# The head of a routed-expert block: the second bias as one row and two matmuls in place of a broadcast transfer

## The chip, the cores and the metric

The kernel runs on one core of one Trainium2 chip. The metric is device time in microseconds (us) of the whole program, the median of several runs.

## The reference, cut to what matters

The block takes 2048 tokens of width 128 and does three things in a row: an expert layer, a linear attention with its own small layer, and the same expert layer again. The expert layer, with `x` the normalised tokens, 8 experts, hidden width 512 and one expert per token:

```
logits = x @ router_W + router_b
probs  = softmax(logits);  gates = one_hot(argmax(probs)) * probs
h = relu(x @ W1[e] + b1[e])          # 512 wide
y = h @ W2[e] + b2[e]                # 128 wide
out = sum over e of gates * y
```

`b2` holds 8 rows of 128 numbers, one per expert: 4 KB. All data is float32.

## The kernel before, in words

The tokens are 16 tiles of 128, in 4 groups of 4 tiles. **Head.** SP issues, one after the other on its own queue, the four groups of `x` (256 KB each, line 411), `rb` (412), the first bias as 32 rows `eb1r` (413), the second bias `b2` (414), the first expert weights of 2 MB (415) and five of eight second weights of 256 KB each (416, helper at 372). The tile `ew` holds, for each partition and expert, W1, b1, b2 and W2 side by side; `B2_AT:W2_AT` is the piece for b2. Line 414 reads the 4 KB of b2 once for each of the 128 partitions, so 512 KB arrive. VectorE (DVE) takes statistics of each group (`begin0`), GpSimd (POOL) makes the reciprocal deviations (542) and a row of constants, TensorE (PE) turns each group by four transposes (`turn_xn`, 951) into a PSUM bank, and ScalarE (ACT) copies that bank to SBUF (`take_xn`, 729). PE then makes the router logits of the group (`logits`, 982). In the first two rounds of that loop (lines 1148 to 1156) stands a `keep_warm(1)`: one bf16 matmul of 512 columns whose result in bank 2 nobody reads. After group 1 PE turns `eb1r` (1156), which DVE copies to `ew` (1604).

**Routing.** DVE picks an expert per token in two halves (`pick(0, 0, 2)`, `pick(0, 2, 2)`, lines 1342 to 1366; each ends in the one-hot tile `oh`). PE's `ranks` (985 to 1017) waits for the first half and for ten constants of POOL, then counts; inside it a `keep_warm(1)` stands between the first half's counts and the `hits` matmul (1004). `tile_list`, a register load of the list of experts, and `sources` (1085) follow; DVE's `list_sources` (1391) writes `srcu`, the row numbers of each tile of the sorted list of 23 tiles.

**Gathers.** Meanwhile ACT (and POOL for group 2, line 589) makes the normalised rows `xn` (`renormalise`, 786) and ACT stores each group to DRAM (`store_xn`, 794, on ACT's queue). POOL then waits for the four stores (622), for `srcu` (623), and gathers the rows of one tile after another by indirect transfers (617). SP loads each tile's W1, b1 and b2 from `ew` into a ring of 8 (`load_weights`, 424), after `ew_in` (both loads into `ew`) and `ebias_ready`.

**Experts.** For each of the 23 tiles PE transposes the gathered rows (1103), multiplies by W1 (1110) and W2 (1127); ACT does the ReLU (755), DVE adds b2 (1473) from the ring. Attention and the second expert layer follow; there b2 is read from `ew` again, halved by POOL (701). Which work goes where and in which order is written out by hand; each engine follows its own list.

Of the kernel before, what the change touches and what calls it, by code (L numbers as in the profile page):

```python
# [5 lines left out]
P = 128  # L6
D = 128
# [5 lines left out]
NG = T // GT  # L13
NE = 8
F = 512
FC = F // P
# [40 lines left out]

W1_AT, B1_AT, B2_AT, W2_AT, EW = 0, F, F + FC, F + FC + D, F + FC + D + FC * D
CW = W2_AT


def bc(ap, shape):
# [3 lines left out]
def macaron_kernel(nc, x_d, g1_d, b1_d, wq_d, wk_d, wv_d, wo_d, g2_d, b2_d, w1_d, w2_d,  # L66
# [3 lines left out]
    ALU, ACT, AX = mybir.AluOpType, mybir.ActivationFunctionType, mybir.AxisListType.X  # L70
# [14 lines left out]
    with ctx:  # L85
# [3 lines left out]
        def sem(name):  # L89
            return ctx.enter_context(nc.semaphore(name))  # L90
# [3 lines left out]
        xi = sb("xi", [P, T, D])  # L94
# [118 lines left out]
        w_in = sem("w_in")  # L213
        ffw_in = sem("ffw_in")
        ew_in = sem("ew_in")
        const_ready = sem("const_ready")
        pool_chain = sem("pool_chain")
        dve_chain = sem("dve_chain")
        ebias_ready = sem("ebias_ready")
        rwmean_ps = sem("rwmean_ps")  # L220
        rwc_ready = sem("rwc_ready")
        eb1_T = sem("eb1_T")
        stats_ready = sem("stats_ready")
        rstd_ready = sem("rstd_ready")
        shift_ready = sem("shift_ready")
# [182 lines left out]
        @block.sync  # L408
        def _(sp):
            for g in range(NG):  # L410
                sp.dma_start(x[:, g * GT:(g + 1) * GT, :], x_v[:, g, :, :]).then_inc(x_in[g], 16)
            sp.dma_start(rb[:, :], rb_d.unsqueeze(0).broadcast_to([P, NE])).then_inc(rb_in, 16)
            sp.dma_start(eb1r[:, :], eb1_d.rearrange("e (c p) -> (e c) p", p=P)).then_inc(eb_in, 16)
            sp.dma_start(ew[:, :, B2_AT:W2_AT], eb2_d.unsqueeze(0).broadcast_to([P, NE, D])).then_inc(ew_in, 16)
            sp.dma_start(ew[:, :, W1_AT:W1_AT + F], ew1_d.rearrange("e p f -> p e f")).then_inc(ew_in, 16)
            load_w2(sp, range(NE - W2_BY_ACT))
            attention_weights = [(gb[:, j:j + 1], v.rearrange("(d a) -> d a", a=1))
                                 for j, v in enumerate((g1_d, b1_d, g2_d, b2_d))]
            attention_weights += [(wkv[:, 0:D], wk_d), (wkv[:, D:2 * D], wv_d), (wq[:, :], wq_d), (wo[:, :], wo_d),
                                  (w1[:, :], w1_d), (w2[:, :, :], w2_d.rearrange("(c p) d -> p c d", p=P))]  # L420

            def load_weights(t, e):

                sp.dma_start(ewc[t.ahead], ew[:, bass.ds(e, 1), 0:CW].squeeze(1)).then_inc(ewc_in[t.ahead], 16)

            def store_slots(k):

                sp.dma_start(slot_scr_v[:, k, :], ysb[:, k, :]).then_inc(y_stored[group_of(k)], 16)

            sp.wait_ge(whole_ready, 1)  # L430
            codes = load_list(sp, codei[0:1, 0:NT], NE * TPE - 1)
            sp.wait_ge(ew_in, 16 * 2)
            sp.wait_ge(ebias_ready, 1)
            for k in range(NT):
                t = Tile(k)
                if k == 1:
                    sp.wait_ge(g_in[0], 16)
                if k >= FIRST:
                    sp.wait_ge(xg_T, max(1, k - LEAD))
                if k >= UNROLL:  # L440
                    sp.wait_ge(y_ready, 1 + k - UNROLL)
                    store_slots(k - UNROLL)
                load_weights(t, expert_of(codes[k]))
            for n, k in enumerate(range(NT - UNROLL, NT)):
                sp.wait_ge(y_ready, 1 + k)
                store_slots(k)
                for out, src in attention_weights[2 * n:2 * n + 2]:
                    sp.dma_start(out, src).then_inc(w_in if n < 4 else ffw_in, 16)

            sp.wait_ge(fill_ready, FILL_PARTS)  # L450
            sp.wait_ge(yb_in[NG - 1], 16 * GT)
            for at in range(0, FILL, T * D):
                n = min(T * D, FILL - at)
                sp.dma_start(row_fill_v[:, at:at + n], xn[:, :, :].rearrange("p t d -> p (t d)")[:, 0:n]).then_inc(fill_done, 16)

            sp.wait_ge(list_ready, 1)
            first = load_list(sp, lists[0:1, 1, 0:FIRST], NE - 1)
            sp.wait_ge(b2_halved, 1)
            for k in range(FIRST):
                load_weights(Tile(k), first[k])  # L460
            sp.wait_ge(codes_ready, 1)
            codes = load_list(sp, lists[0:1, 0, 0:NT], CODES - 1)
            for k in range(FIRST, NT):
                t = Tile(k)
                if k == FIRST + 1:
                    for g in range(NG):
                        sp.wait_ge(scattered[g], 16 * GT)
                    for n in range(SURE, UNROLL):
                        load_rows(sp, Tile(n), codes[n])
                if k >= UNROLL:  # L470
                    sp.wait_ge(out_done[t.ahead], 16 * t.round)
                    load_rows(sp, t, codes[k])
                    sp.wait_ge(o_ready, 1 + k - UNROLL)
                sp.wait_ge(xg_T, NT + max(1, k - LEAD))
                load_weights(t, expert_of(codes[k]))
            for u in range(UNROLL):
                sp.wait_ge(out_done[u], 16 * uses(u))
# [246 lines left out]
        def _(act):  # L724
            A = nc.scalar.activation

            def take_xn(m, g):
                act.wait_ge(xnT_ps, m * NG + g + 1)
                A(xnT[:, g * GT:(g + 1) * GT, :], bank[xn_bank(m, g)][:, :], ACT.Copy).then_inc(xnT_ready, 1)

            def take_last_xn():

                for n, bk in enumerate((0, 4)):
                    act.wait_ge(xnT_ps, 2 * NG + n)
                    A(xnT[:, T - GT + 2 * n:T - GT + 2 * n + 2, :], bank[bk][:, 2 * n * P:(2 * n + 2) * P], ACT.Copy
                      ).then_inc(xnT_ready, 1)

            def exponentials():
                act.wait_ge(lg_ready, picks(0))
                A(ex[:, :, :], lg[:, :, :], ACT.Exp).then_inc(ex_ready, 1)  # L740
# [41 lines left out]
            def renormalise(g):  # L782

                act.wait_ge(shift_ready, g + 1)
                for t in range(g * GT, (g + 1) * GT):
                    last = A(xn[:, t, :], x[:, t, :], ACT.Identity, scale=rstd[:, t, 0:1], bias=shift[:, t, 0:1])
                last.then_inc(xn_ready, 1)

            def store_xn(g):
                if g == POOL_ROWS:  # L790
                    act.wait_ge(xn_by_pool, 1)
                else:
                    act.wait_ge(xn_ready, 1 + g - (g > POOL_ROWS))
                act.dma_start(xn_scr_v[:, g, :, :], xn[:, g * GT:(g + 1) * GT, :]).then_inc(xn_stored[g], 16)
# [12 lines left out]

            act.dma_start(rw[:, :], rw_d).then_inc(rw_in, 16)
            nc.scalar.preload_act_table_set("natural_log_exp_and_others")
            for g in range(NG):  # L810
                take_xn(0, g)
            renormalise(0)
            renormalise(1)
            store_xn(0)
            store_xn(1)
            renormalise(3)
            store_xn(3)
            store_xn(POOL_ROWS)
# [109 lines left out]
        def _(pe):  # L928
# [11 lines left out]
            def turn_xn(m, g):  # L940
# [11 lines left out]
                                               pay[:, t, 0:D] if m else x[:, t, :], ident[:, :])  # L952
                last.then_inc(xnT_ps, 1)

            def turn_last(j):

                pe.wait_ge(x3_ready, x3_count(B - 1, j))
                if j == 0:
                    pe.wait_ge(xnT_ready, 2 * NG - 1)
                turned = nc.tensor.transpose(bank[0 if j < 2 else 4][:, j * P:(j + 1) * P],  # L960
                                             pay[:, T - GT + j, 0:D], ident[:, :])
                if j % 2 == 1:
                    turned.then_inc(xnT_ps, 1)
# [21 lines left out]
            def ranks():  # L985
# [13 lines left out]
                mm(R[:, 0:PICKED * NE], before[:, :], oh[:, 0:PICKED, :], start=False, stop=False, skip_group_check=True)  # L999
                for t in range(PICKED):  # L1000
                    spread(t)
                keep_warm(1)
                pe.wait_ge(oh_ready, picks(0))
                mm(bank[4][:, 4:5], oh[:, :, :].rearrange("p t e -> p (t e)"), ones_bf[:, 0:1], start=True, stop=True
# [138 lines left out]

            turn_xn(0, 0)
            pe.wait_ge(rw_in, 16)
            mm(bank[4][:, 0:NE], avg[:, :], rw[:, :], start=True, stop=True).then_inc(rwmean_ps, 1)
            turn_xn(0, 1)
            for g in range(NG):
                if g + 2 < NG:
                    turn_xn(0, g + 2)  # L1150
                if g < 2:
                    keep_warm(1)
                logits(0, g)
                if g == 1:
                    pe.wait_ge(eb_in, 16)
                    nc.tensor.transpose(bank[7][:, 0:NE * FC], eb1r[:, :], ident[0:NE * FC, 0:NE * FC]).then_inc(eb1_T, 1)
            ranks()
            tile_list()
            keep_warm(5)
# [157 lines left out]
        def _(dve):  # L1317
# [273 lines left out]
            v.tensor_scalar(sums[:, :, :], sums[:, :, :], 1.0 / P, None, ALU.mult).then_inc(sums_ready, 1)  # L1591
            begin0(0)
            begin0(1)
            dve.wait_ge(rwmean_ps, 1)
            v.tensor_tensor(out=rwc[:, :], in0=rw[:, :], in1=bank[4][:, 0:NE], op=ALU.subtract).then_inc(rwc_ready, 1)
            first_shift(0)
            begin0(2)
# [2 lines left out]
            dve.wait_ge(rb_in, 16)  # L1600
            pick(0, 0, 2)
            first_shift(2)
            dve.wait_ge(eb1_T, 1)
            v.tensor_copy(ew[:, :, B1_AT:B2_AT], bank[7][:, 0:NE * FC].rearrange("p (e c) -> p e c", c=FC)
                          ).then_inc(ebias_ready, 1)
            pick(0, 2, 2)
# [188 lines left out]
```

## Time and profile before

| what | value |
|---|---|
| median of 3 runs | 205.19 us (204.97 to 207.0) |
| the profiled execution | 204.63 us |
| its span, first to last instruction | 202.9 us |
| PE, POOL, DVE, ACT busy | 185.8, 121.6, 122.7, 111.7 us |
| mean granted TensorE clock | 0.966 |

A chain of waits is read backwards from the last instruction; in the timeline a row is a start, a duration, an engine, a line and, in brackets, the idle time before it and what ended it. A float32 matmul shows as two matmul instructions. [...]

### The profile page before, as it was taken

What the parts mean: (1) busy time and instruction counts of PE and PEld (TensorE: products, weight loads), DVE (VectorE), ACT (ScalarE), POOL (GpSimd) and SP (SyncE); (2) the same over time, 40 slices, a digit from 0 to 9 for tenths busy, and PEclk for the clock granted to TensorE, in tenths of its full rate; (3) what the DMA queues carried; (4) which work ended last, traced back from release to release, by engine and by line L of the source; (5) the groups of instructions that cost most, each with busy time, mean ns of one, the idle gap of its engine ahead of it and who ended that gap; (6) DMA issues with size and microseconds to landing.
All of it is one profiled execution on the core that took longest, in us unless ns stands there. A gap on an engine that the chain in (4) does not pass through costs nothing.

```text
span 202.9 us, 4566 instructions
## 1 busy us (share of the span) xinstructions
PE 185.8 (92%) x1410; PEld 156.9 (77%) x1410; DVE 122.7 (60%) x521; ACT 111.7 (55%) x326; POOL 121.6 (60%) x186
## 2 busy tenths in 40 slices
PE   4969879999999998998999999998998999999992
PEld 2854358999999986777855868797545999999991
DVE  4868412222222888898897484876515677777762
ACT  2675026556556658787878852510302766766670
POOL 6887656587774576361887440858771354554554
PEclk9975599999999999999999999999999999999999
DMA  6999869767698562599990000011047867674700
GB/s 204 233 387 345 263 220 365 262 216 237 207 193 301 140 178 53 198 417 413 415 393 14 2 3 0 30 42 47 28 134 254 287 247 265 225 261 159 272 29 0
DMA packets 26680, 40.26 MB, mean 198 GB/s; under 512 B 4229, under 2 KB 16296, under 8 KB 25632
## 3 DMA queue, kind: packets, MB, share of 16 engines
q1 hardware_dynamic: 21136, 33.01, 46.2%
q0 software_dynamic: 2496, 4.76, 8.9%
q10 hardware_dynamic: 3024, 2.20, 3.5%
q8 instruction: 12, 0.20, 0.4%
q14 instruction: 12, 0.10, 0.1%
HBM read 10.78 MB, written 14.46 MB: 124 GB/s over the span
## 4 chain that ended last, share of the span: by engine, by line
PE 60%; DVE 17%; DMA 8%; POOL 7%; issue 4%; ACT 1%; ACTq 1%; POOLq 0%; DVEq 0%
PE bank L1110 18%; PE bank L1127 17%; PE bank L1248 7%; PE bank L1266 5%; DMA Xg<-xn_scratch,srcu 4%; PE bank L1103 3%; DMA xn_scratch<-xn 2%; PE bank L1201 2%; DMA eqrq<-row_scratch 2%; PE bank L934 2%; DVE stat L1335 2%; POOL xn L589 2%; PE bank L1211 1%; DVE x L1577 1%; PE bank L1218 1%
## 5 line engine op out<-in xcount | busy, mean ns | idle before, releaser
L755 ACT ACTIVATE hT<-bank,ewc_own 128x128 f32<-128x128 f32 x184 | 52.3, 368 | 48.9 <-PE bank L1110 48.8
L1110 PE MATMUL bank<-xT,ewc_own 128*128 128x128 f32 x368 | 48.7, 275 | 0.4 <-DVE xT L1467 0.3
L1127 PE MATMUL bank<-ew,hT 128*128 x368 | 48.5, 275 | 0.0
L1110 PEld LDWEIGHTS bank<-xT,ewc_own 128*128 128x128 f32 x368 | 44.7, 192 | 1.2 <-issue 1.2
L1127 PEld LDWEIGHTS bank<-ew,hT 128*128 128x128 f32 x368 | 44.7, 192 | 0.2 <-issue 0.2
L689 POOL DMA_INDIRECT out_dram<-ysb,eqrq x23 | 22.6, 983 | 25.4 <-DVE ysb L1477 25.1
L617 POOL DMA_INDIRECT Xg<-xn_scratch,srcu x23 | 22.0, 958 | 11.0 <-issue 5.8
L934 PE MATMUL bank<-ones_bf 128*128 128x512 bf16 x66 | 21.7, 464 | 3.1 <-POOL ident L507 2.7
L681 POOL DMA_INDIRECT row_scratch<-pay,posu x16 | 15.8, 987 | 11.0 <-DVE posu L1440 7.4
L1473 DVE TENSOR_TENSOR ysb<-bank,ewc_own 128x128 f32<-128x128 f32 x23 | 6.6, 289 | 26.0 <-PE bank L1127 24.6
L642 POOL DMA_INDIRECT xnT<-slot_scratch,posu x16 | 15.3, 958 | 9.4 <-DMA slot_scratch<-ysb 2.9
L1467 DVE COPY xT<-bank 128x128 f32<-128x128 f32 x46 | 13.1, 284 | 7.6 <-PE bank L1103 7.5
L1266 PE MATMUL bank<-w,actT 128*128 128x128 f32 x128 | 16.3, 278 | 0.0
L1103 PE MATMUL bank<-ident,Xg 128*128 128x128 f32 x46 | 12.8, 278 | 2.7 <-DMA Xg<-xn_scratch,srcu 1.9
L934 PEld LDWEIGHTS bank<-ones_bf 128*128 128x128 bf16 x66 | 6.9, 114 | 10.6 <-issue 5.0
L1266 PEld LDWEIGHTS bank<-w,actT 128*128 128x128 f32 x128 | 15.1, 192 | 0.0
L1248 PE MATMUL bank<-h1T,w 128*128 128x512 f32 x32 | 14.4, 592 | 0.0
L1477 DVE SCALAR_TENSOR_TENSOR ysb<-bank,gate,ysb 128x128 f32<-128x128 f32 x23 | 8.1, 351 | 9.6 <-PE bank L1127 8.9
L871 ACT ACTIVATE actT<-ewc_own 128x512 f32<-128x512 int16 x16 | 9.3, 622 | 8.0 <-DVE ewc_own L1678 8.0
L1486 DVE TENSOR_SCALAR Xg<-eqrq 128x128 f32<-128x128 f32 x23 | 7.9, 341 | 5.1 <-DMA eqrq<-row_scratch 5.0
L1248 PEld LDWEIGHTS bank<-h1T,w 128*128 128x128 f32 x32 | 5.8, 190 | 5.7 <-issue 5.5
L1678 DVE TENSOR_SCALAR ewc_own<-bank 128x512 int16<-128x512 f32 x16 | 10.0, 683 | 0.1
(240 smaller groups left out, 302.8 us busy)
## 6 DMA issues: line engine op xcount, KB each, us to landing
ewc_own<-ew SPq DMA_DIRECT2D x46, 322.0 KB, 3.4
row_scratch<-xn SPq DMA_DIRECT2D x8, 1024.0 KB, 10.6
ew<-in_L_ffn_W_dram SPq DMA_DIRECT2D x1, 2048.0 KB, 12.2
slot_scratch<-ysb SPq DMA_DIRECT2D x23, 64.0 KB, 3.3
ew<-in_L_ffn_W_dram SPq DMA_DIRECT2D x5, 256.0 KB, 9.3
eqrq<-row_scratch SPq DMA_DIRECT2D x18, 70.0 KB, 2.4
x<-in_L_attn_x_dram SPq DMA_DIRECT2D x4, 256.0 KB, 3.2
xn_scratch<-xn ACTq DMA_DIRECT2D x4, 256.0 KB, 5.7
```

What stands on the lines that cost most here:

```text
L617: g.indirect_dma_start(out=Xg[:, k % UNROLL, :], out_offset=None, in_=xn_scr, in_offset=bass.IndirectOffsetOnAxis(ap=srcu[:, k:k + 1], axis=0)
L642: g.indirect_dma_start(out=Yg[:, t, :], out_offset=None, in_=slot_scr[0:UPTO[group] * P, :], in_offset=bass.IndirectOffsetOnAxis(ap=posu[: ...
L681: g.indirect_dma_start(out=row_scr, out_offset=bass.IndirectOffsetOnAxis(ap=posu1[:, t:t + 1], axis=0), in_=pay[:, t, :], in_offset=None). ...
L689: g.indirect_dma_start(out=out_rows, in_=ysb[:, k, :], in_offset=None, bounds_check=TOK - 1, oob_is_err=False, out_offset=bass.IndirectOff ...
L755: last = A(hT[:, t.slot, c * P:(c + 1) * P], up_bank(k, c)[:, c * P:(c + 1) * P], ACT.Relu, scale=0.5 if m else 1.0, bias=ewc[t.ahead][:, ...
L934: mm(bank[2][:, :], ones_bf[:, :], bc(ones_bf[:, :].unsqueeze(1), [P, 4, P]), start=True, stop=True)
L1103: nc.tensor.transpose(bank[t.parity][:, 0:P], Xg[:, t.ahead, :], ident[:, :]).then_inc(xg_T, 1)
L1110: last = mm(up_bank(k, c)[:, c * P:(c + 1) * P], ewc[t.ahead][:, c * P:(c + 1) * P], xT[:, t.slot, :], start=True, stop=True)
L1127: last = mm(bank[4 + t.parity][:, 0:D], hT[:, t.slot, c * P:(c + 1) * P], ew[:, bass.ds(e[k], 1), W2_AT + c * D:W2_AT + (c + 1) * D].squee ...
L1248: mm(hidden_bank(c)[:, :], w1[:, c * P:(c + 1) * P], h1T[:, b % 2, :], start=True, stop=True).then_inc(u_ps, 1)
L1266: last = mm(row_bank(b, j)[:, j * P:(j + 1) * P], actT[:, b % 2, c, j * P:(j + 1) * P], w2[:, c, :], start=c == 0, stop=c == FC - 1)
L1467: v.tensor_copy(xT[:, t.slot, :], bank[t.parity][:, 0:P]).then_inc(xT_ready, 1)
```

## The change

Line 414 now loads b2 as one row of 4 KB into `xi`, a tile that is free until the attention, and counts on `eb_in` beside `eb1r`; `ew_in` counts the W1 load alone. PE spreads the row over the partitions by two float32 matmuls with a row of ones as weights (512 columns each, four experts at a time, into bank 2), and ACT copies bank 2 into `ew`. The first pair stands in round 0 of the logits loop and on ACT ahead of the copy of the last group, the second after that loop and on ACT after the first two stores are issued. The two `keep_warm(1)` of the loop are gone. The semaphores `rwmean_ps` and `eb1_T` become one, `small_ps`, which counts the router mean, the first spread, the turned `eb1r` and the second spread in PE's order.

```diff
-            sp.dma_start(ew[:, :, B2_AT:W2_AT], eb2_d.unsqueeze(0).broadcast_to([P, NE, D])).then_inc(ew_in, 16)
+            sp.dma_start(xi[0:1, 0:NE, :], eb2_d.unsqueeze(0)).then_inc(eb_in, 16)
...
-            sp.wait_ge(ew_in, 16 * 2)
+            sp.wait_ge(ew_in, 16)
+            sp.wait_ge(eb2_ready, 2)
...
+            def take_b2(n):
+                act.wait_ge(small_ps, 2 * (n + 1))
+                A(ew[:, n * HALF_E:(n + 1) * HALF_E, B2_AT:W2_AT], bank[2][:, :].rearrange("p (e d) -> p e d", d=D), ACT.Copy
+                  ).then_inc(eb2_ready, 1)
...
-            for g in range(NG):
+            for g in range(NG - 1):
                 take_xn(0, g)
+            take_b2(0)
+            take_xn(0, NG - 1)
             renormalise(0)
             renormalise(1)
             store_xn(0)
             store_xn(1)
+            take_b2(1)
             renormalise(3)
...
+            def spread_b2(n):
+                pe.wait_ge(eb_in, 16 * 2)
+                if n == 1:
+                    pe.wait_ge(eb2_ready, 1)
+                mm(bank[2][:, :], ones_v[0:1, :], xi[0:1, n * HALF_E:(n + 1) * HALF_E, :].rearrange("p e d -> p (e d)"),
+                   start=True, stop=True).then_inc(small_ps, 1)
...
                 for t in range(PICKED):
                     spread(t)
+                pe.wait_ge(eb2_ready, 2)
                 keep_warm(1)
...
-                if g < 2:
-                    keep_warm(1)
+                if g == 0:
+                    spread_b2(0)
                 logits(0, g)
                 if g == 1:
-                    pe.wait_ge(eb_in, 16)
-                    nc.tensor.transpose(bank[7][:, 0:NE * FC], eb1r[:, :], ident[0:NE * FC, 0:NE * FC]).then_inc(eb1_T, 1)
+                    pe.wait_ge(eb_in, 16 * 2)
+                    nc.tensor.transpose(bank[7][:, 0:NE * FC], eb1r[:, :], ident[0:NE * FC, 0:NE * FC]).then_inc(small_ps, 1)
+            spread_b2(1)
             ranks()
...
-            dve.wait_ge(eb1_T, 1)
+            dve.wait_ge(small_ps, 3)
```

## Rows read from the trace of the kernel before

**Rows 1.** Chain of waits, 16 to 40 us: start, duration, what.
```profile
16.54 4.97 DMA xn_scratch<-xn
...
22.08 0.04 POOLq L623
...
25.77 3.35 DMA Xg<-xn_scratch,srcu
...
29.50 0.92 PE bank L1110 x8
...
30.44 0.02 POOLq L612
```

**Rows 2.** Transfers of line 794, the store issued last alone.
```profile
L794 ACTq DMA_DIRECT2D xn_scratch<-xn x1: 327/327/327, 16.5 to 16.5; - x1
...
DMA to landing us min/median/max: 5.5/5.5/5.5
```

**Rows 3.** Timeline of DVE in the head: start, duration, line, operation.
```profile
9.83 0.23 DVE L1349 TENSOR_TENSOR lg<-bank,rstd 128x64 f32<-128x64 f32 x1 [0.49 <-PE bank L982]
...
13.26 0.22 DVE L1365 TENSOR_TENSOR oh<-key,kmax 128x64 bf16<-128x64 f32 x1
...
21.67 0.18 DVE L1391 TENSOR_SCALAR srcu<-bank 128x23 uint32<-128x23 f32 x1 [0.99 <-PE bank L1085]
```

**Rows 4.** Issues of transfers up to 45 us: queue, count, KB, us to landing.
```profile
ew<-in_L_ffn_b_dram SPq DMA_DIRECT2D x1, 512.0 KB, 6.3
...
eb1r<-in_L_ffn_b_dram SPq DMA_DIRECT2D x1, 16.0 KB, 3.2
```

**Rows 5.** Timeline of SP's queue, 3 to 21 us.
```profile
3.14 0.43 SPq L413 DMA_DIRECT2D eb1r<-in_L_ffn_b_dram  x1
3.62 0.42 SPq L414 DMA_DIRECT2D ew<-in_L_ffn_b_dram  x1
...
20.74 11.02 SPq L424 DMA_DIRECT2D ewc_own<-ew  x8
```

**Rows 6.** Stretches: engines' busy us and counts, then granted clock, DMA share, GB/s.
```profile
5.00:9.00 4.00, 3.83 (x33) 3.55 (x31) 3.73 (x24) 2.13 (x4) 3.39 (x6) 1.00 0.97 194
9.00:12.00 3.00, 2.69 (x23) 2.53 (x22) 2.27 (x15) 3.00 (x9) 2.35 (x8) 1.00 1.04 393
12.00:13.00 1.00, 0.00 (x0) 0.00 (x0) 0.87 (x4) 0.32 (x1) 0.71 (x5) 0.62 1.07 414
13.00:25.00 12.00, 10.72 (x65) 5.50 (x66) 7.03 (x30) 4.88 (x13) 9.16 (x19) 0.50 1.02 320
```

**Rows 7.** The page's costliest groups: the float32 matmul of 512 columns, later in the kernel.
```profile
L1248 PE MATMUL bank<-h1T,w 128*128 128x512 f32 x32 | 14.4, 592 | 0.0
```

**Rows 8.** Timeline of PE in the head.
```profile
6.96 0.38 PE L934 MATMUL bank<-ones_bf 128*128 128x512 bf16 x1
7.17 0.95 PE L982 MATMUL bank<-rwc,xnT 128*128 128x8 f32 x8
...
8.67 0.95 PE L982 MATMUL bank<-rwc,xnT 128*128 128x8 f32 x8
...
9.73 1.95 PE L982 MATMUL bank<-rwc,xnT 128*128 128x8 f32 x16
13.23 0.23 PE L990 MATMUL bank<-ones_v,whole 1*32 1x1 f32 x2 [1.54 <-POOL token L583]
...
14.37 0.61 PE L934 MATMUL bank<-ones_bf 128*128 128x512 bf16 x1
14.78 0.21 PE L1004 MATMUL bank<-ones_bf,oh 128*128 128x1 bf16 x1
14.92 0.61 PE L1006 MATMUL bank<-tileid,ones_v 1*128 1x23 f32 x2
```

**Rows 9.** Timeline of ACT in the head.
```profile
8.66 0.60 ACT L729 ACTIVATE xnT<-bank 128x512 f32<-128x512 f32 x1 [0.90 <-PE bank L951]
...
13.60 1.65 ACT L786 ACTIVATE xn<-x,shift,rstd 128x128 f32<-128x128 f32 x4 [1.28 <-DVE shift L1385]
```

More of the change, by code:

```diff
@@ L59 @@
 CW = W2_AT
+HALF_E = NE // 2
 def bc(ap, shape):
@@ L215, in macaron_kernel @@
         ew_in = sem("ew_in")
+        small_ps = sem("small_ps")
+        eb2_ready = sem("eb2_ready")
         const_ready = sem("const_ready")
@@ L219, in macaron_kernel @@
         ebias_ready = sem("ebias_ready")
-        rwmean_ps = sem("rwmean_ps")
         rwc_ready = sem("rwc_ready")
-        eb1_T = sem("eb1_T")
         stats_ready = sem("stats_ready")
@@ L1145, in _ @@
             pe.wait_ge(rw_in, 16)
-            mm(bank[4][:, 0:NE], avg[:, :], rw[:, :], start=True, stop=True).then_inc(rwmean_ps, 1)
+            mm(bank[4][:, 0:NE], avg[:, :], rw[:, :], start=True, stop=True).then_inc(small_ps, 1)
             turn_xn(0, 1)
@@ L1593, in _ @@
             begin0(1)
-            dve.wait_ge(rwmean_ps, 1)
+            dve.wait_ge(small_ps, 1)
             v.tensor_tensor(out=rwc[:, :], in0=rw[:, :], in1=bank[4][:, 0:NE], op=ALU.subtract).then_inc(rwc_ready, 1)
```

## Prediction, made before the changed kernel was run

> **What bounds the kernel now.** I read the chain of waits first. From 36 us on it is TensorE (PE) work nearly back to back, which the change doesn't touch; the head is what counts. There the chain goes through the last store of normalised rows, POOL's gathers and PE's first expert tiles [rows 1]. What delays the first gather delays the gathers behind it, PE's first tiles, and so the end, one for one.
>
> What releases the first gather? The store that is issued last starts at 16.54 and lands 5.5 us later, at 22.04 [rows 2]. POOL's record of the wait behind it, the one for `srcu`, stands at 22.08 [rows 1]. DVE finishes `srcu` at 21.67 + 0.18 = 21.85 [rows 3]. How long after its release such a record stands is seen further down: PE ends at 29.50 + 0.92 = 30.42, POOL's record is at 30.44 [rows 1]. So 22.08 fits a release at 22.04 and is 0.23 too late for one at 21.85. The store is the last wait, by 0.2 us only, and the routing that ends in `srcu` stands right behind it. That is the main reading: two paths, almost level, and the change helps one and touches the other.
>
> Second, the routing path. PE's `ranks` starts at 13.23 after 1.54 of idle time, released by POOL's constants, not by DVE; the `hits` matmul at 14.78 follows in PE's own order, while the second half of the one-hot tile was ready at 13.26 + 0.22 = 13.48 [rows 3, 8]. So PE has slack before 13.23, DVE has 1.3 us before 14.78, and work added on PE ahead of `ranks` is free up to 13.23 and costs one for one beyond.
>
> Third, the clock. It is 1.00 to 12 us, 0.62 on average from 12 to 13, and 0.50 after, up to 25 [rows 6]. A mean of 0.62 between 1.00 and 0.50 is 0.24 us at the upper level: it fell at 12.24, after PE went idle at 9.73 + 1.95 = 11.68 [rows 8].
>
> **The change part by part.** *Removed: the broadcast.* From 5 to 9 us the transfer engines are 97% busy yet move 194 GB/s; from 9 to 12 it is 393 [rows 6]. 4 us at 194 are 776 KB; less the 524 KB of the broadcast, 252 KB remain, 0.65 us at 393. So the broadcast took about 4 x 0.97 - 0.65 = 3.2 us of all engines. Were it as quick as the later transfers, 524 / 393 = 1.3. The transfers behind it move up by 1.3 to 3.2 us, I take 3.2, the row of its own stretch. The engines are full from 13 to 25 as well (share 1.02), so the last store feels it: it should land between 18.8 and 20.7 instead of 22.04. But only 0.2 of that is worth anything: after it `srcu` is late next. Gain: 0.2 us, with 0 as its other end.
>
> *Added on SP: one row.* It stands where the broadcast stood, so nothing is moved past a queue. Issued at 3.62 [rows 5], it should take what `eb1r`, 0.48 ahead of it in the same queue and four times as large, took: 3.2, landing at 6.8; the upper end is the broadcast's own 6.3, landing at 9.9 [rows 4]. PE arrives at 6.96 [rows 8]. I take 6.8 and no wait. SP's new wait for both copies stands ahead of its first weight load at 20.74 [rows 5]; the copies are done six us earlier (below): 0.
>
> *Added on PE: the first spread, in place of two warmers.* A float32 matmul of 512 columns is two instructions; 32 take 14.4 us, 0.45 each, and one lasts 592 ns to its end [rows 7]. So a spread holds PE for 0.90 and its result is there after 1.04. It starts at 6.96, where a warmer held PE for 7.17 - 6.96 = 0.21 [rows 8]: +0.69 for what follows. In the next round the other warmer's 0.21 goes: +0.48 from there on. The logits of group 3 end at 12.16 instead of 11.68; DVE's first pick starts at 10.3 instead of 9.83. Its cover is the 1.3 us before `hits`: 0.
>
> *Added on PE: the second spread.* It starts at about 12.05, as the last small matmul leaves PE. If the clock falls at 12.24 as now, 0.19 of its 0.90 run at the upper level and the other 0.71 take 1.42: PE is held to 13.66, the result is there at about 13.8. `ranks` starts at 13.66 instead of 13.23: **+0.43**. The ends: clock still up, 12.95, nothing; clock down before it, 12.05 + 1.80 = 13.85, +0.6. I take 0.43, since the fall is where the row has it.
>
> *Added on ACT.* The first copy (0.60, as a `take_xn` [rows 9]) runs from 8.0 to 8.65; the turned group 3 comes at 8.66 + 0.69 = 9.35 anyway, so it delays nothing by itself. The second waits for the second spread at 13.8 and ends at about 14.45. Behind it wait the rows of group 3, at 14.45 instead of 13.60 [rows 9], so its store is issued at 16.1; the last store still goes at 16.54, when POOL's rows are ready. Cover: 0.1 us of queue, and behind that the 1.3 to 3.2 us by which stores land earlier: 0. PE's new wait for this copy stands ahead of the warmer at 14.37 [rows 8], now 14.8, with `hits` queued behind it: 0.35 us of cover. DVE's wait for the turned `eb1r` is over by 10.3, before its pick ends: 0.
>
> *Sum.* `srcu` 0.43 later is 22.28; POOL passes at 22.30 instead of 22.08: +0.43 - 0.2 = **+0.2 us**, between -0.2 (second spread free) and +0.6 (clock down earlier, and no relief). Against the profiled execution that is 204.63 + 0.2 = 204.8. The median of the runs shown stands 0.56 above that execution, at 205.19, so I say 205.4.
>
> **The rivals.**
> 1. *The clock falls early, slower.* The warmers held the clock, and without them it falls before the logits are done. If it falls at t, all PE work from t to 12.05 takes twice its time and the second spread 1.80, so `ranks` starts at 13.85 + (12.05 - t). Less 0.2 of relief, the loss passes 1% (2.05 us) when t is before 10.4; at t = 9.0 it is 0.6 + 3.05 - 0.2 = 3.4, 208.6 us. For: the warmers are PE work that nothing else needs, and their columns are gone. Against: the first spread streams for 0.90 where the two warmers streamed for 0.43, and the clock held from 9 to 12 with only small matmuls and transposes [rows 6, 8]. [...] Chance 0.10.
> 2. *The row lands late, slower.* If it lands at 9.9, PE waits 3.0 ahead of all logits; the second spread then runs at the lower level from 15.05, and `ranks` starts at 16.85: +3.4, 208.6. It decides from a landing at 6.96. For: the engines are 97% busy there [rows 6]. Against: `eb1r`, just ahead, landed at 6.34 [rows 4, 5]. Chance 0.05.
> 3. *The clock stays up, faster.* [...] With the store out of the way, -0.2 - 0.4: 204.6. Chance 0.12.
> 4. *The relief does not reach the store.* Other transfers fill the room, it still lands at 22.04. With `srcu` at 22.28 the sum is the same 205.4; with a free second spread no change, 205.2. Chance 0.07.
>
> My forecast keeps 0.66.
>
> **How the numbers follow.** About 1% is what a measurement of this kernel tells from no change. Rivals 3 and 4 and the forecast lie within it. Slower by more: most of 1 and 2, 0.12. Faster by more needs rival 3 and something unseen, say every early gather landing sooner: 0.04. The range reaches from rival 3 less the 0.2 by which runs fall under the median, 204.4, to a clock fall around 11 us (0.6 + 1.05 - 0.2 = 1.45), 206.7; left out are the early fall and the late row, and a little on both sides, not quite 0.2.
>
> **What would show it.** Right: the last store lands before 21 us; POOL's record for `srcu` stands right behind DVE; `ranks` starts near 13.7, and the second spread's two instructions last longer than the first's; the first gather within 0.4 us of where it was and the rest shifted by the same. Wrong: a PE idle stretch before the first spread (row late); a granted clock below 1.00 before 11 us; a `hits` matmul that waits for ACT's second copy; or an end that moves by more than the first gather does, for then the experts' stage has a limit that I have not seen.

## The result, and the profile after

The changed kernel takes 207.82 us (median of 4 runs, 207.3 to 209.57) against 205.67 us for the kernel before on the same chip (4 runs, 204.97 to 207.0): ratio 1.0125 [1.0066, 1.0183], 1.2% slower. The forecast was 205.4 us, with 206.7 as the upper end. The profiled execution took 207.68 us, with a span of 206.0 us, 3.1 us more than the 202.9 us of the one before. Here and below a ratio leaves out the runs that lie over 1.5% above the fastest run of their own kernel, while a median is over all runs, so a ratio can differ from the quotient of the two medians.

Everything is lost ahead of the first gather. This is the end of the head in the chain of waits of the changed kernel (start, duration, what), in answer to [rows 1]:

```profile
11.58 3.42 PE bank L1001 x16
15.00 2.00 PE bank L971 x2
17.00 0.19 PE bank L1009 x2
...
25.40 0.19 DVE srcu L1412
25.59 0.02 issue
25.61 0.04 POOLq L625
25.66 0.84 issue
26.50 1.25 POOL Xg L619
...
32.88 0.92 PE bank L1130 x8
```

POOL's record of its wait for `srcu` now stands right behind DVE (25.61, with `srcu` done at 25.59). No store is the last wait any more. The first gather starts at 26.50; in the kernel before it stood here:

```profile
22.97 1.25 POOL Xg L617
```

The first expert tile's eight matmuls start at 32.88 instead of 29.50 [rows 1]: +3.4, so the end moves by no more than the first gather and first tile do. The same holds for every trace kept of this case: in all 14 of them the span ends 179.1 to 180.3 us after the first gather starts, wherever between 22.97 and 28.14 that is. The stage behind is nearly the same in both kernels. These are the busy times of PE, PE's weight loads, DVE, ACT and POOL with counts, then clock, DMA share and GB/s, of the kernel after and, in the second fence, of the kernel before, in stretches shifted with the gather:

```profile
36.00:204.00 168.00, 160.24 (x1246) 139.44 (x1244) 105.18 (x432) 97.53 (x292) 97.83 (x118) 1.00 0.54 185
```

```profile
32.50:201.00 168.50, 160.18 (x1247) 139.53 (x1245) 105.23 (x432) 97.63 (x292) 97.97 (x118) 1.00 0.54 184
```

PE's timeline of the changed kernel's head (start, duration, line, operation; a bracket gives idle time and its releaser), in answer to [rows 8]:

```profile
5.96 1.95 PE L962 MATMUL bank<-ident,x 128*128 128x128 f32 x8
7.84 1.29 PE L971 MATMUL bank<-xi,ones_v 1*128 1x512 f32 x2
9.06 1.06 PE L1001 MATMUL bank<-rwc,xnT 128*128 128x8 f32 x8
...
10.44 0.96 PE L1001 MATMUL bank<-rwc,xnT 128*128 128x8 f32 x8
...
11.51 3.50 PE L1001 MATMUL bank<-rwc,xnT 128*128 128x8 f32 x16
14.93 2.07 PE L971 MATMUL bank<-xi,ones_v 1*128 1x512 f32 x2
16.93 0.26 PE L1009 MATMUL bank<-ones_v,whole 1*32 1x1 f32 x2
...
18.51 0.21 PE L1024 MATMUL bank<-ones_bf,oh 128*128 128x1 bf16 x1
```

L971 is the spread, L1001 the logits, L1009 the first matmul of `ranks`, L1024 the `hits` matmul. Each spread is one float32 matmul of the program and two instructions of this trace (x2), the four logits matmuls of a group are eight (x8), while the eight float32 transposes of L962 are eight (x8). No line up to `hits` has a bracket: PE doesn't wait from 2.72 us on, and the 1.54 us ahead of `ranks` [rows 8] are gone. The second spread takes 2.07, the first 1.29. The stretches around the clock's fall (columns as above), in answer to [rows 6]:

```profile
11.00:12.00 1.00, 1.00 (x8) 0.94 (x7) 0.36 (x2) 1.00 (x4) 0.63 (x4) 0.82 1.03 398
12.00:13.00 1.00, 1.00 (x7) 1.00 (x6) 0.86 (x5) 1.00 (x4) 0.71 (x5) 0.50 1.10 353
```

A mean of 0.82 between 1.00 and 0.50 is 0.64 us at the upper level: the clock fell to 0.50 at 11.64, with half of the logits and the whole second spread still to come. ACT's timeline, in answer to [rows 9]:

```profile
17.04 0.60 ACT L743 ACTIVATE ew<-bank 128x512 f32<-128x512 f32 x1 [2.73 <-PE bank L971]
17.53 1.63 ACT L794 ACTIVATE xn<-x,shift,rstd 128x128 f32<-128x128 f32 x4
19.20 0.81 ACTq L802 DMA_DIRECT2D xn_scratch<-xn x2
```

Ahead of the copy of the second spread ACT stands idle for 2.73 us, waiting for PE, and the last two stores leave behind it at 19.20 and about 19.6. They land 4.0 and 4.2 us after their issue (the first two took 5.0 and 5.2), so the last is there at about 23.8, still ahead of `srcu`.

### The profile page after: what moved, and what is told of

It is laid out like the page before. It is cut to its first block, busy times and chain, and to the rows that moved or that the text cites. A ratio compares the mean times of both kernels' runs of the same rounds, so it can differ in the third digit from the quotient of the medians.

```text
span 206.0 us, 4573 instructions
## 1 busy us (share of the span) xinstructions
PE 191.0 (93%) x1412; PEld 160.0 (78%) x1412; DVE 123.1 (60%) x521; ACT 112.8 (55%) x328; POOL 121.4 (59%) x186
## 4 chain that ended last, share of the span: by engine, by line
PE 71%; DVE 15%; POOL 4%; issue 4%; DMA 4%; ACT 1%; POOLq 0%; DVEq 0%
PE bank L1130 18%; PE bank L1147 16%; PE bank L1269 7%; PE bank L945 6%; PE bank L1287 4%; DMA Xg<-xn_scratch,srcu 4%; PE bank L1001 3%; PE bank L1123 3%; PE bank L1222 2%; PE bank L962 2%; PE bank L971 2%; PE bank L1232 1%; DVE x L1598 1%; DVE inr L1399 1%; PE bank L1239 1%
## 5 line engine op out<-in xcount | busy, mean ns | idle before, releaser
L945 PE MATMUL bank<-ones_bf 128*128 128x512 bf16 x64 | 20.5, 457 | 3.1 <-POOL ident L509 2.7
```

Source lines behind the costliest of these rows:

```text
L945: mm(bank[2][:, :], ones_bf[:, :], bc(ones_bf[:, :].unsqueeze(1), [P, 4, P]), start=True, stop=True)
```

## The experiments

My theory after the result: the loss is the two spreads, as PE work ahead of `ranks`, together with the clock's course; the transfers have no part in it. Against it stood that the transfers in their new order do the harm, that it is the missing warmers alone, and that the profiled execution of the kernel before was not typical. Each ratio is against the kernel before on the same chip. The diffs of b_nowarm, b_nowarm2 and b_early are against the kernel before, the others against the changed one. Where a trace is shown, it is of one execution.

**b_again: the kernel before, unchanged.**

```diff
(no edit)
```

> The kernel before, unchanged, for a second profile of it. Three theories for the 2.2 us that the change cost. Order: the two spreads are PE work on PE's own list ahead of the routing, and what was idle there is used up. Warmers: without the two warmers the clock falls before the logits are done. Phase: the clock's rise and fall come at other times in every execution, and the one profile of before happened to have an early rise. Order and warmers expect 205 to 206 us, ranks starting near 13.2 us and the logits of group 3 done by 12. Phase expects this profile to show transposes at the lower rate (four in over 0.8 us) near 6 us or a granted clock that falls before 12, with ranks late by a microsecond or more.

205.13 us (10 runs; 25 of the kernel before beside it), 0.9992 [0.9949, 1.0035], as it should be. What it is for is its trace. PE's timeline:

```profile
5.96 1.95 PE L951 MATMUL bank<-ident,x 128*128 128x128 f32 x8
7.70 0.63 PE L934 MATMUL bank<-ones_bf 128*128 128x512 bf16 x1
8.13 1.10 PE L982 MATMUL bank<-rwc,xnT 128*128 128x8 f32 x8
...
9.77 0.95 PE L982 MATMUL bank<-rwc,xnT 128*128 128x8 f32 x8
...
10.83 2.69 PE L982 MATMUL bank<-rwc,xnT 128*128 128x8 f32 x16
13.45 0.26 PE L990 MATMUL bank<-ones_v,whole 1*32 1x1 f32 x2
...
15.46 0.19 PE L1004 MATMUL bank<-ones_bf,oh 128*128 128x1 bf16 x1 [0.21 <-DVE oh L1365]
...
21.69 0.58 PE L1085 MATMUL bank<-inq,inr 128*128 128x23 f16 x16 [1.05 <-DVE inr L1378]
```

Its clock around the fall (columns as above), and the end of its head in the chain of waits:

```profile
11.00:12.00 1.00, 1.00 (x10) 1.00 (x10) 0.86 (x5) 1.00 (x4) 0.66 (x4) 0.92 1.05 393
```

```profile
22.52 0.04 POOLq L623
...
23.40 1.25 POOL Xg L617
```

The same program has no idle time ahead of `ranks` here, and `hits` waits for DVE. A mean of 0.92 puts the clock's fall at 11.84. The record of the wait for `srcu` stands at 22.52, right behind DVE, which finishes `srcu` at 22.50: in this execution the store is not the last wait. Its transposes (L951) take 1.95 for eight; in the execution that I predicted from they stood like this:

```profile
4.82 0.89 PE L951 MATMUL bank<-ident,x 128*128 128x128 f32 x4
...
5.69 0.63 PE L951 MATMUL bank<-ident,x 128*128 128x128 f32 x4
```

0.63 for four is 1.26 for eight. So PE came up to its upper rate about 5.5 us into that execution, an estimate from the 0.89 between 1.06 and 0.63, and over 2 us later in this one, where the warmer at 7.70 still takes 0.63. Of what Phase expected of this trace, the slow transposes and the fall ahead of 12 are there; the late `ranks` is not: 13.45 against 13.23.

**b_both: the changed kernel with the broadcast kept beside the row** (the two copies write to an unused part of `xi`, so that nothing but the relief is missing).

```diff
+            sp.dma_start(ew[:, :, B2_AT:W2_AT], eb2_d.unsqueeze(0).broadcast_to([P, NE, D])).then_inc(ew_in, 16)
...
-                A(ew[:, n * HALF_E:(n + 1) * HALF_E, B2_AT:W2_AT], bank[2][:, :]...
+                A(xi[:, NE + n * HALF_E:NE + (n + 1) * HALF_E, :], bank[2][:, :]...
```

> The change without its relief: the broadcast transfer stays, and the row, the two spreads and ACT's two copies are there as well (the copies go to a part of xi that nobody reads); the two warmers are out. Order and warmers expect what the changed kernel has, 207.3 to 208.3 us with ranks starting near 17 us, and so a relief worth 0 to 0.3 us. If instead the row's transfer or the missing broadcast itself does the harm (transfers that start later, engines left idle at 6 us), this comes out within 0.7 us of the kernel before.

207.74 us (10 runs), 1.0091 [1.0058, 1.0123]: as slow as the change, within the intervals. The loss is there with the broadcast in place, so the missing broadcast is not what costs. A gain from leaving it out could not show here: in this trace too `srcu` is the last wait (done at 25.47, POOL's record at 25.49).

**a_late: the row and the spreads kept, but the spreads moved behind the routing**, where they replace five warmers, in two banks of their own; the loop's two warmers stand again, and ACT copies after its weight loads.

```diff
-                if g == 0:
-                    spread_b2(0)
+                if g < 2:
+                    keep_warm(1)
                 logits(0, g)
...
-            spread_b2(1)
             ranks()
             tile_list()
-            keep_warm(5)
+            pe.wait_ge(ebias_ready, 1)
+            spread_b2(0)
+            spread_b2(1)
```

> The changed kernel with the row kept and no broadcast, but the two spreads moved behind the routing, in place of five warmers (banks 7 and 1), ACT's copies behind its row hits; the two warmers of the logits loop are back. Order: the loss is gone, 205.0 to 205.8 us, ranks near 13.2, and the broadcast's relief shows as at most 0.2 us of gain. Warmers expects the same. Phase expects it between the two, 206 to 207.5.

204.91 us (10 runs), 0.9954 [0.9917, 0.9991]. The whole loss is won back, and the interval lies just below the kernel before. PE's timeline, with the late rise of b_again:

```profile
5.96 1.95 PE L961 MATMUL bank<-ident,x 128*128 128x128 f32 x8
...
10.74 2.77 PE L998 MATMUL bank<-rwc,xnT 128*128 128x8 f32 x16
13.44 0.26 PE L1006 MATMUL bank<-ones_v,whole 1*32 1x1 f32 x2
...
18.28 3.76 PE L968 MATMUL bank<-xi,ones_v 1*128 1x512 f32 x4
21.97 0.60 PE L1101 MATMUL bank<-inq,inr 128*128 128x23 f16 x16
```

`ranks` is where b_again has it (13.44, 13.45). The two spreads take 3.76 at 18.28, almost all of it in time in which PE only kept warm: the matmuls of `sources` start right behind them at 21.97, in b_again at 21.69 after 1.05 of waiting for DVE. So 0.28 us of the spreads is still on the path in this trace. The row is loaded here as in the changed kernel and the broadcast is gone, and the loss is gone too: the transfers are not its cause.

**a_warm: the changed kernel with the two warmers back** (bank 7), spreads in place.

```diff
+                if g < 2:
+                    warm7()
                 if g == 0:
                     spread_b2(0)
```

> The changed kernel, spreads where they are, with the two warmers back in the first two rounds of the logits loop (into bank 7). Warmers: the clock holds to past 12 us, ranks start before 14.5 us, 205.5 to 206.3 us. Order: nothing is won, 0.2 to 0.4 us more PE work ahead of the routing, 207.5 to 208.5 us, ranks at 16 us or later.

207.26 us (4 runs: 204.83, 205.91, 208.61 and 209.38), and no ratio: two runs are where the kernel before is and two where the changed kernel is, so what the warmers give back stays unsettled. The trace is of the 205.91 us run. In it the transposes took 1.48 for eight and the clock held until about 13.6:

```profile
11.29 1.95 PE L1005 MATMUL bank<-rwc,xnT 128*128 128x8 f32 x16
13.18 1.64 PE L975 MATMUL bank<-xi,ones_v 1*128 1x512 f32 x2
14.75 0.26 PE L1013 MATMUL bank<-ones_v,whole 1*32 1x1 f32 x2
```

b_both had the same rise (5.96 1.48) without the warmers, and its clock stood at 0.61 on average from 10 to 11. A second pair with equal rise (eight transposes in 1.33) says the same: with the warmers and no spread the clock fell at 13.0 (b_early, below), with the spreads and no warmers at 9.5 (a_early). But b_nowarm, without warmers and without spreads, held it to 12.3, and a_one, with warmers and one spread, only to 11.0. So single executions suggest that the warmers hold the clock up; they don't prove it. Even here `ranks` comes 1.5 us later than in [rows 8].

**a_again: the changed kernel, unchanged.**

```diff
(no edit)
```

> The changed kernel, unchanged, timed beside the others on one chip and with a second profile. Order and warmers: 207.0 to 208.3 us; ranks between 15 and 17.2 us, by when the clock falls in this execution. Phase (the first profile was an unlucky one): below 206.5.

208.4 us (4 runs, 207.78 to 210.52), 1.0173 [1.0084, 1.0262], and nearly the same trace as the first time (the second spread at 14.93 for 2.07, `ranks` at 16.93). The loss repeats.

**a_one: warmers back, only the first spread in the loop, the second behind `tile_list`.**

```diff
+                if g < 2:
+                    warm7()
                 if g == 0:
                     spread_b2(0)
...
-            spread_b2(1)
             ranks()
             tile_list()
-            keep_warm(5)
+            spread_b2(1)
+            keep_warm(1)
```

> Of the two spreads only the first stays in the logits loop, both warmers are back (bank 7), and the second spread is behind the routing. Order: the first spread takes about 1 us of PE ahead of the logits, the second one took 2 us right ahead of ranks; so ranks start between 13.2 and 14.7 us and the time is 205.2 to 206.4, nearer to the kernel before than to the changed one. If the first spread does the harm by itself (it delays logits and picks), 206.8 to 208.

207.85 us (10 runs), 1.0126 [1.0087, 1.0166]. The first spread alone, which I had priced at nothing, costs as much as both. Against a_late, which has warmers in the loop as well, the place of this one spread is the main difference (1.0126 and 0.9954). In the trace of its profiled execution the clock fell at about 11 and the logits ran into it:

```profile
10.59 1.37 PE L1005 MATMUL bank<-rwc,xnT 128*128 128x8 f32 x8
...
12.13 3.58 PE L1005 MATMUL bank<-rwc,xnT 128*128 128x8 f32 x16
15.64 0.26 PE L1013 MATMUL bank<-ones_v,whole 1*32 1x1 f32 x2
```

Against b_again the last logits start 1.30 later (12.13, 10.83) and take 3.51 instead of 2.62, so `ranks` is 2.19 late and the first gather 2.13 (25.53, 23.40).

**a_second: the other half alone: warmers back, the second spread ahead of `ranks`, the first behind.**

```diff
-                if g == 0:
-                    spread_b2(0)
+                if g < 2:
+                    keep_warm(1)
                 logits(0, g)
...
             spread_b2(1)
             ranks()
             tile_list()
-            keep_warm(5)
+            spread_b2(0)
+            keep_warm(1)
```

> The mirror of the kernel with only the first spread in the loop: both warmers back, the second spread in its place ahead of ranks, the first behind the routing. [...] Clock: the warmers hold it as in before, the loss stays under 1 us, 205.2 to 206.3.

206.91 us (10 runs), 1.0041 [1.0000, 1.0082]. In the profiled execution the whole spread stands on the path:

```profile
10.73 2.79 PE L998 MATMUL bank<-rwc,xnT 128*128 128x8 f32 x16
13.45 2.07 PE L968 MATMUL bank<-xi,ones_v 1*128 1x512 f32 x2
15.45 0.26 PE L1006 MATMUL bank<-ones_v,whole 1*32 1x1 f32 x2
```

`ranks` is 2.00 us later than in b_again. The first gather is 1.61 later (25.01, 23.40), since `hits` no longer waits for DVE. The medians stand 1.25 us apart (206.91, 205.66); by the ratio it is 0.4%, or 0.8 us.

**b_nowarm and b_nowarm2: the kernel before without the loop's two warmers**, one kernel on two chips.

```diff
-                if g < 2:
-                    keep_warm(1)
                 logits(0, g)
```

> The kernel before with the two warmers of the logits loop taken out and nothing else. Warmers: the clock falls before the logits are done and the time is 206.3 to 208 us. Order: PE's work ahead of ranks is still short enough for its slack, 204.8 to 205.9 us, though the clock may fall earlier than with them.

> The kernel before without its two warmers a second time, for a profile of a slower execution (the first profile, 205.29 us, was its fastest). Clock: such an execution shows transposes near 6 us at the lower rate, a granted clock that falls again before 12, and ranks or hits late by a microsecond or more; median 206.3 to 208.5. If the warmers work in another way (on the experts' stage), ranks stand near 13.3 and the time is lost behind the first gather.

The first: 207.44 us (4 runs), 1.0118 [1.0038, 1.0197]. The second: 205.73 us (10 runs), 0.9976 [0.9932, 1.0019]; one of its runs took 311.73 us at a mean clock of 0.562. The first trace is of that kernel's fastest run (205.29 us): `ranks` at 13.32 after 2.02 us of idle time. The second is of one of the slowest (207.47 us), with `ranks` at 15.55 and no idle time, and it cannot be set beside the others: PE's rate did not come up ahead of `ranks` at all.

```profile
7.70 1.72 PE L982 MATMUL bank<-rwc,xnT 128*128 128x8 f32 x8
```

These eight logits matmuls take 0.95 at the upper rate [rows 8]. What the two warmers are worth stays open, and with it how much of the change's loss is theirs.

**b_early, a_early and a_late_early: three more warmers at PE's start**, ahead of those that wait for POOL's constants, in the kernel before, the changed one and a_late, meant to bring the rate up early in every execution.

```diff
+            pe.wait_ge(pool_chain, 2)
+            keep_warm(3)
             pe.wait_ge(const_ready, 2)
             keep_warm(5)
```

> The kernel before with the three more warmers at the start, beside which the late spreads with the same warmers (204.73) can be read. Clock: it always rises early, 204.3 to 205.2 us and a narrower spread of runs than before's. If the broadcast costs nothing, level with the late spreads with early warmers; if its relief is worth something, 0.2 to 0.5 us slower than those.

> The changed kernel as it is (both spreads in place, the two warmers out), with three more warmers at the very start of PE. It tells the clock from PE's order. [...] Order: the spreads' work on PE is too long at either rate: 206.6 to 208.3.

> The late spreads, and three more warmers at the very start of PE, which wait only for the tile of ones and not for the identity. If the late rise of the clock costs the head something, the transposes near 6 us run at the upper rate in this profile, ranks start at 13.2 and the time is 203.9 to 204.7. If PE's slack already hides that rise: as the late spreads alone, 204.6 to 205.2.

b_early: 205.87 us (10 runs), 0.9994 [0.9955, 1.0032]. a_early: 209.21 us (4 runs), 1.0124 [1.0032, 1.0216]: an early rise was to bring it back to 205.0 to 206.4, and that did not come. a_late_early: 204.73 us (10 runs), 0.9967 [0.9935, 0.9999], no different from a_late within the intervals, although its `ranks` has 2.02 us of idle time ahead of it and a_late's has none. b_early was expected at 204.3 to 205.2 with a narrower spread of runs; it is level with the kernel before, and its runs reach from 204.92 to 208.37. In a_early's profile, of one of its two slowest runs (210.12 us), PE got to the first spread early and stood idle for the row, and the logits then ran at the lower rate:

```profile
5.96 1.33 PE L964 MATMUL bank<-ident,x 128*128 128x128 f32 x8
7.95 1.12 PE L973 MATMUL bank<-xi,ones_v 1*128 1x512 f32 x2 [0.66 <-DMA xi<-in_L_ffn_b_dram]
9.00 1.43 PE L1003 MATMUL bank<-rwc,xnT 128*128 128x8 f32 x8
...
13.06 3.58 PE L1003 MATMUL bank<-rwc,xnT 128*128 128x8 f32 x16
16.57 2.07 PE L973 MATMUL bank<-xi,ones_v 1*128 1x512 f32 x2
```

So an early rise alone doesn't free the spreads: in this one execution rivals 1 and 2 act together.

## Why the prediction was wrong

**What held.** The end follows the first gather, and the routing behind the stores is next in line. The transfers behind the broadcast do move up: the 2 MB of first weights land 9.4 us after their issue in the changed kernel (10.2 in a_again) instead of 12.2 (11.6 in b_again), 1.4 to 2.8 us less, inside the 1.3 to 3.2 us of the prediction. The relief was put at 0.2 us with 0 as its other end. In b_again it would be nothing, because the store is not the last wait there; in the changed kernel nothing that ends the head waits for a store.

**The step that failed: the overlap, that is the slack on PE before 13.23 and DVE's 1.3 us before `hits`.** With it the second spread was put at +0.43 (0 to +0.6) and the first at 0; the two measured +3.48 at `ranks` together with the logits that they pushed behind the clock's fall. Both terms rest on PE being done with the logits at 11.68 and idle until 13.23 [rows 8]. That idle time was a property of one execution, not of the kernel. b_again shows how: the rate comes up over 2 us later, the first logits start at 8.13 instead of 7.17, the last at 10.83 instead of 9.73, the clock falls before they are done, PE reaches `ranks` at 13.45 without a pause, and `hits` waits for DVE. Against that trace, which has the changed kernel's late rise, the sum comes out:

- the first spread in place of a warmer: first logits at 9.06 instead of 8.13, +0.93; the second warmer gone: last logits at 11.51 instead of 10.83, +0.68 (I had +0.69 and +0.48; the sizes were nearly right, the cover was not there);
- the last logits, more of them behind the fall: 14.93 - 11.51 = 3.42 instead of 13.45 - 10.83 = 2.62, +0.80;
- the second spread, all of it at a granted clock of 0.50: 16.93 - 14.93, +2.00;
- `ranks` therefore at 16.93 instead of 13.45, +3.48; `hits` no longer waits for DVE and follows `ranks` by 1.58 instead of 2.01, -0.43; the first gather at 26.50 instead of 23.40, +3.1, and the span 206.0 instead of 202.5, +3.5. The last 0.4 arise behind the gather, and no run shows where.

The medians stand 2.15 us apart on the first chip (207.82 - 205.67) and 3.09 on a_again's (208.4 - 205.31). b_again's execution, at 204.26 us, equals the fastest of its ten although PE has no slack in it: by this one execution slack is worth nothing to the kernel before, and counts only once work is added. The price of 0.90 for a spread at full rate was a little low: in a_warm the first holds PE for 1.05 (7.58 to 8.63). Half rate for the second stood in the range, at 1.80 for the 2.00 measured, but only from 12.05 on and with the idle time still under it; logits pushed behind the fall stood in no term of the sum, only in rival 1.

**Rival 1** named the mechanism, work at the lower rate, but with the same flaw. Its formula counts from 12.05, the end of PE's work in the early execution. Put in what the changed kernel does: at full rate the last logits would have held PE for 1.89 (as in a_warm, 13.18 - 11.29), to 13.40; with the fall at 11.64 this gives 11.64 + 2 x 1.76 + 2.00 = 17.2 for `ranks`, and 16.93 was measured. The factor 2 was my estimate from 0.50 against 1.00; the same logits held PE for 3.51 in a_early (16.57 - 13.06), all at 0.50, against those 1.89: 1.86 times. I gave the rival 0.10 because I asked only whether the clock falls earlier. In the changed kernel it fell at 11.64 instead of 12.24, hardly earlier; the work was later. In b_both (10.2) and a_early (9.5), which have the same two spreads and no warmers in the loop, it did fall early. So the odds of 0.10 were too low on that count as well, but whether it was for want of the warmers, as the rival has it, is not shown.

**Rival 2**, the late row, has a grain of truth: a_early's spread starts at 7.95 after waiting for the row, so it landed about 4.3 us after its issue at 3.61, not 3.2. The 3.2 was itself one execution's: `eb1r` takes 4.3 in b_again. In the changed kernel PE comes to the spread at 7.84 and shows no wait.

**Rival 3.** The lower end of the range, 204.4, rests on its gain of 0.4 us, and no run shows that gain: in 13 of the 14 traces the clock is at 0.50 from 14 us on, past 17 us, in the other (b_nowarm2) it stands at 1.00, and the warmer ahead of `hits` takes 0.61 to 0.62 in all 14, as in [rows 8].

**Also wrong:** the last store was to land before 21 us. ACT's second copy, priced at nothing, held back the stores of group 3 from 16.1 to 19.2. It cost nothing only because `srcu` was later still.

**What stays open.** How much belongs to the spreads as such and how much to the warmers that they displaced: a_one and a_second say that each spread costs with the warmers there, but their costs do not add up to the change's, and b_nowarm's two results contradict each other. No trace has the changed kernel with the early rise and the late fall that I predicted from. And where a_late's 0.5% comes from: its gather is no earlier than b_again's (23.70 and 23.40), and its interval ends at 0.9991.

## What to carry to other kernels

Idle time read from one execution need not be there in the next: the 1.54 us ahead of `ranks` in the first profile of the kernel before were none in b_again, where PE's rate came up over 2 us later. So take a second profile of the kernel before, and cost the added work from the one in which the engine has the least room. Work that is needed late, such as a bias of a later stage, belongs behind the serial chain that the whole kernel waits for, in place of filler, and not ahead of it: moved there, with the filler of the loop back in place, the same spreads went from 1.2% slower to level or a little faster (0.9954 [0.9917, 0.9991]).

## What the runs showed of the hardware

- The recorded clock does not show PE's rate early in an execution. It stands at 1.00 from 5 to 9 us both where four transposes take 0.63 us (the kernel before) and where eight take 1.95 (b_again, the changed kernel). In b_nowarm2 it stands at 1.00 for the whole span, while the logits of the head take 1.72 for eight instead of 0.95. Durations of equal instructions show the rate; the record shows the later fall, and in b_nowarm2 nothing.
- When the clock falls differs between executions of near-identical heads: at 9.5 us in a_early (0.76 on average from 9 to 10), 10.2 in b_both, about 11.0 in a_one, 11.6 in the changed kernel, 11.8 and 12.2 in two executions of the kernel before, 13.6 in a_warm.
- In a_early the row of 4 KB took about 4.3 us, although from 6 to 8 us, the stretch in which PE came to wait for it, the transfer engines were 20% busy (columns as above):

```profile
6.00:8.00 2.00, 1.33 (x10) 0.88 (x10) 1.83 (x15) 1.71 (x3) 1.73 (x4) 1.00 0.20 38
```
